# Eight-core layer kernel: the recurrent fronts of the first two tiles run back to back on weights kept in SBUF, with tile two's out-projection placed in the first attention

## The reference, cut to what matters

```python
n  = layernorm(x)
xp = silu(n @ W_in.T)
a  = sigmoid(xp @ W_alpha.T + b_alpha)
b  = sigmoid(xp @ W_beta.T + b_beta)
v  = tanh(xp @ W_v.T + b_v)
h[t] = a[t] * h[t-1] + (b*v)[t]             # a scan over the 4096 tokens
x1 = x + (h * silu(h)) @ W_out.T
n1 = layernorm(x1)
hh = rmsnorm(n1) * gamma1
q  = hh @ Wq + bq ;  k, v = split((hh @ Wdown + bdown) @ Wup + bup)
att = softmax(q_heads @ k_heads.T / 8)      # 16x16, among the heads of one token
u  = n1 + att @ v @ Wo + bo
h2 = rmsnorm(u) * gamma2
g  = softmax(h2 @ Wg + bg)                  # 8 experts, dense
out = x1 + u + sum_e g[e] * (h2 @ We[e])
```

## Time and profile before

| what | value |
|---|---|
| median of 3 runs | 2030.08 us (lowest 2024.43) |
| profiled execution, its own time | 2033.6 us |
| its span, slowest core | 2031.8 us (eight cores: 2020.7 to 2031.8 us) |
| PE busy | 1902.7 us, 94% |
| DVE busy | 1273.2 us, 63% |
| ACT busy | 736.9 us, 36% |
| POOL busy | 219.8 us, 11% |
| HBM read, written | 318.65 MB, 48.23 MB |

### The profile page before, as it was taken

The page is one execution under the profiler, slowest core; times in us unless marked ns, Lnnn a source line. Parts: engine busy times, 40 slices in busy tenths (PEclk is TensorE's granted clock), DMA queues, the critical chain, the costliest instruction groups (busy, mean ns, idle before and its releaser), DMA issues.

```text
span 2031.8 us, 32594 instructions; the slowest of 8 cores (2020.7 to 2031.8 us)
## 1 busy us (share of the span) xinstructions
PE 1902.7 (94%) x11200; PEld 909.7 (45%) x11200; DVE 1273.2 (63%) x2170; ACT 736.9 (36%) x1969; POOL 219.8 (11%) x222
## 2 busy tenths in 40 slices
PE   4666699999999999999999999999999999999899
PEld 2223344445444454455444554444544554444444
DVE  2448546866478646776468665786467764676544
ACT  2226442533434333542325334443335423352200
POOL 4543100120002100020001100021000200011000
PEclk9877799999999999999999999999999999999999
DMA  8999987665533363434543355333543344423344
GB/s 246 301 320 204 152 200 200 163 170 177 192 129 126 124 229 127 161 113 160 203 149 123 120 187 192 108 146 124 208 151 139 125 156 156 145 105 125 125 145 166
DMA packets 49582, 334.89 MB, mean 165 GB/s; under 512 B 6016, under 2 KB 6016, under 8 KB 14592
## 3 DMA queue, kind: packets, MB, share of 16 engines
q1 hardware_dynamic: 42176, 271.45, 38.6%
q0 software_dynamic: 7248, 61.36, 13.4%
HBM read 318.65 MB, written 48.23 MB: 181 GB/s over the span
## 4 chain that ended last, share of the span: by engine, by line
PE 80%; DMA 8%; DVE 7%; issue 3%; ACT 1%; POOL 1%; DVEq 0%; SPq 0%; ACTq 0%; POOLq 0%
PE bank L352 39%; PE bank L407 14%; PE bank L421 6%; PE bank L535 6%; PE bank L392 5%; DVE kt L801 4%; DMA we<-wall 3%; DMA we<-wscr 3%; PE bank L485 2%; DVE R L807 2%; PE bank L520 2%; PE bank L510 1%; PE bank L453 1%; DMA wscr<-wm 1%; PE bank L434 1%
## 5 line engine op out<-in xcount | busy, mean ns | idle before, releaser
L352 PE MATMUL bank<-we,h2T 128*128 128x512 bf16 x4096 | 940.3, 380 | 16.0 <-DMA we<-wscr 7.9
L705 DVE SCALAR_TENSOR_TENSOR xs<-bank,gat,xs 128x512 f32<-128x512 f32 x512 | 384.1, 750 | 411.7 <-PE bank L352 410.3
L352 PEld LDWEIGHTS bank<-we,h2T 128*128 128x128 bf16 x4096 | 385.9, 98 | 441.9 <-issue 29.4
L407 PE MATMUL bank<-F,wm 128*128 128x512 bf16 x1536 | 339.3, 383 | 21.5 <-POOL wm L274 20.6
L287 POOL TENSOR_TENSOR pb<-pb,sml 128x512 bf16<-128x512 bf16 x128 | 133.2, 1040 | 1410.5 <-DVE sml L824 1410.5
L660 ACT ACTIVATE pb<-bank,sml 128x128 bf16<-128x128 f32 x512 | 181.2, 371 | 206.1 <-DVE sml L816 206.1
L407 PEld LDWEIGHTS bank<-F,wm 128*128 128x128 bf16 x1536 | 151.3, 99 | 208.4 <-issue 32.0
L760 DVE SCALAR_TENSOR_TENSOR R<-R 128x512 f32<-128x512 f32 x64 | 47.0, 735 | 123.9 <-ACT R L612 123.9
L421 PE MATMUL bank<-wm,F 128*128 128x512 bf16 x512 | 114.5, 385 | 10.2 <-POOL wm L274 10.2
L453 PE MATMUL bank<-F,wm 128*128 128x512 bf16 x512 | 121.5, 380 | 0.0
L535 PE MATMUL bank<-wm,F 128*128 128x512 bf16 x512 | 113.6, 383 | 0.7 <-DVE F L853 0.7
(11 more groups left out here) (84 smaller groups left out, 1666.0 us busy)
## 6 DMA issues: line engine op xcount, KB each, us to landing
we<-wscr SPq DMA_DIRECT2D x128, 1024.0 KB, 5.2
wm<-wscr SPq DMA_DIRECT2D x98, 1024.0 KB, 5.9
wscr<-wall POOLq DMA_DIRECT2D x16, 1024.0 KB, 15.1
out<-xs SPq DMA_DIRECT2D x32, 512.0 KB, 3.0
wscr<-wm POOLq DMA_DIRECT2D x14, 1024.0 KB, 25.4
xs<-x SPq DMA_DIRECT2D x7, 2048.0 KB, 10.4
xs<-wall POOLq DMA_DIRECT2D x12, 1024.0 KB, 22.9
we<-wall POOLq DMA_DIRECT2D x10, 1024.0 KB, 22.8
```

The source lines that it names most:

```text
L352: mm = pe.matmul(b[:, :], hT[:, kc * 512 + tb * 128:kc * 512 + (tb + 1) * 128], we[ui % NE][:, kc * 512:(kc + 1) * 512], start=(kc == 0), ...
L407: mm = pe.matmul(bk[(mc % 2) * 3 + j][:, :], w[:, (ci % 4) * 1024 + kc * 128:(ci % 4) * 1024 + (kc + 1) * 128], F2[:, kc * 512:(kc + 1) * ...
L705: v.scalar_tensor_tensor(dst, bk[6 + k % 2][:, :], gat[(t - 1) % 2][:, tb * 8 + e:tb * 8 + e + 1], dst, OP.mult, OP.add).then_inc(v_ec, 1)
```

## The change

1. Order. PE, ACT and DVE run t1(0), win(0), abv(0), t1(1), win(1), wout(0), abv(1), wq(0), attention(0), t2(1), wo(0), wdn(1), t3(0), gate(0), and then wq(1), attention(1) and the rest of tile 1 with the experts' units of tile 0 in between. t2(0) and wdn(0) lie inside abv(1). Tiles 2 to 7 keep their order.
2. wout(1), eight groups of eight matmuls, sits in steps j = 0 to 7 of attention(0), with DVE's two instructions of each (`x1ev`) in the same step; the normalization of tile 1 follows in steps 8 to 14.
3. Weights. All 14 units of tiles 0 and 1 are cast once into a buffer of their own (`w0s`: h2T, wm, halves of qt and kt, we[0]) and used for both tiles. Units 0 to 9 are loaded without a wait for PE or for a write-back; units 10 to 13 reuse the buffers of 0 to 3. The write-backs move from POOL to SP and start when unit 9 is cast. Four staging buffers in place of five. x of tile 1 is loaded once unit 0 is cast.
4. `ce(e)` starts after unit 13 and is spread anew, up to `ce(15)` in attention(1).
5. In the fronts of tiles 2 to 7 the 32 transposes on PE and the four copies on DVE are replaced by four DMA transposes on SP's queue, SBUF to SBUF, 128x1024 bf16 each, issued after wo(t-1) and its two weight loads.
6. Three we buffers in place of two (pb and ptv now lie in F2). In wq two units of experts (after mc 2 and 5) in place of one, in wo two in place of three, and in tile 1 sixteen at the end.

The diff, cut to its core:

```diff
-NE = 2
+NE = 3
-A_WIN, A_ABV, A_WOUT, A_T2, A_S0, A_WO, A_T3, A_GATE = 2, 4, 7, 1, 2, 3, 7, 2
+A_WIN, A_ABV, A_WOUT, A_T2, A_S0, A_WO, A_T3, A_GATE = 2, 4, 7, 1, 3, 2, 7, 2
...
+A_END1 = NEC - (A_S0 + A_ATT + A_WO + A_T3 + A_GATE)
...
-    stgh = [xs[2][:, 0:2048], xs[2][:, 2048:4096]] + [t[:, :].bitcast(F32) for t in (h2T[1], we[0], we[1])]
+    stgh = [xs[2][:, 0:2048], xs[2][:, 2048:4096]] + [t[:, :].bitcast(F32) for t in (we[1], we[2])]
+    w0s = [h2T[1], wm[1], wm[2], wm[0], qt[:, 0:4096], qt[:, 4096:8192], kt[:, 0:4096], kt[:, 4096:8192],
+           we[0], h2T[0], h2T[1], wm[1], wm[2], wm[0]]
...
@@ sp_prog
+        def wb(u):
+            sync.wait_ge(c_cm, 2 * u + 2)
+            sync.dma_start(out=wscr[u * 128:(u + 1) * 128, :], in_=w0s[u][:, 0:4096]).then_inc(s_cv[u], 16)
...
+        sync.wait_ge(c_cm, 2)
+        load_x(1)
+        sync.wait_ge(c_cm, 20)
+        for u in range(NMU):
+            wb(u)
...
+        for i in range(NE):
+            load_e(i)
...
             sync.wait_ge(p_wo, t * 8 + 8)
             load_m(m0 + 16)
-            ec(t, A_T3 + A_GATE + A_END)
+            if t + 1 < NT:
+                for b in range(NB):
+                    sync.wait_ge(a_l1a, (t + 1) * 4 + b + 1)
+                    sync.dma_start(out=F1[:, :].rearrange("p (k n) -> p k n", n=TT)[:, :, b * 128:(b + 1) * 128],
+                                   in_=tm1[:, b * D:(b + 1) * D], transpose=True).then_inc(s_t1, 16)
+            ec(t, A_T3 + A_GATE + (A_END1 if t == 1 else A_END))
...
@@ pool_prog
         def cm(u):
-            f = u - NM
-            if f >= 0:
...
-                gp.wait_ge(s_cv[f], 16)
             for hf in range(2):
                 h = 2 * u + hf
-                gp.wait_ge(s_ld[h % 5], 16 * (h // 5 + 1))
-                gp.tensor_copy(wm[u % NM][:, hf * 2048:(hf + 1) * 2048], stgh[h % 5]).then_inc(c_cm, 1)
+                gp.wait_ge(s_ld[h % 4], 16 * (h // 4 + 1))
+                gp.tensor_copy(w0s[u][:, hf * 2048:(hf + 1) * 2048], stgh[h % 4]).then_inc(c_cm, 1)
...
-            gp.dma_start(out=wscr[u * 128:(u + 1) * 128, :], in_=wm[u % NM][:, :]).then_inc(s_cv[u], 16)
...
+        for u in range(10):
+            cm(u)
...
+        gp.wait_ge(p_win, 8 + 4)
+        gp.wait_ge(s_cv[0], 16)
+        cm(10)
...
+        gp.wait_ge(p_abv, 24 + 8)
+        gp.wait_ge(s_cv[3], 16)
+        cm(13)
         ce(0)
+        gp.wait_ge(p_abv, 24 + 16)
         ce(1)
...
@@ pe_prog
+        pe.wait_ge(s_c1, 48)
+        t1(0)
+        win(0)
+        abv(0)
+        t1(1)
+        win(1)
+        for u in range(8):
+            wout(0, u)
+        abv(1)
+        wq(0)
+        att(0)
+        t2(1, range(4))
+        wo(0)
+        wdn(1)
+        t3(0)
+        gate(0)
+        for t in range(1, NT):
+            if t >= 2:
+                win(t)
...
+            wq(t)
+            att(t)
...
+        def att(t):
...
+                if t >= 1:
+                    ec(t, 1)
+                elif j < 8:
+                    wout(1, j)
...
@@ dve_prog
+        def att(t):
...
+                if t == 0 and j < 8:
+                    x1ev(1, j)
+                if j + 1 < 16:
+                    rsum(t, j + 1)
...
+        wo(0)
+        v.drain()
+        xu(0)
+        nb3(0)
+        t3(0)
```

More of the change, by code:

```diff
@@ L689, in act_prog @@
             r.then_inc(a_ge, 1)
+        load_set(SET_LNE)
+        s.wait_ge(v_set, 1)
+        ln1_rstd(0)
+        for b in range(NB):
+            ln1_app(0, b)
+        load_set(SET_SILU)
+        win(0)
+        abv(0)
+        win(1)
+        load_set(SET_LNE)
+        ln2_rstd(0)
+        load_set(SET_SILU)
+        for b in range(NB):
+            ln2_app(0, b)
+        abv(1)
+        load_set(SET_LNE)
+        qv(0)
+        att(0)
+        ln3(0)
+        zev(1)
+        gate(0)
+        for t in range(1, NT):
+            if t >= 2:
+                load_set(SET_SILU)
+                win(t)
+                abv(t)
+                load_set(SET_LNE)
+                ln2_rstd(t)
+                for b in range(NB):
+                    ln2_app(t, b)
+                zev(t)
+            qv(t)
+            att(t)
+            ln3(t)
+            gate(t)
     def dve_prog(v):
@@ new lines, in t3 @@
+        def t3(t):
+            for kc in range(NCH):
+                if kc % 2 == 0:
+                    v.wait_ge(p_t3, t * 4 + kc // 2 + 1)
+                if t < 2 and kc == 0:
+                    v.wait_ge(s_cv[9 + t], 16)
+                bb = bkb[(4, 5, 0, 1)[kc // 2]]
+                v.tensor_scalar_mul(h2T[t % 2][:, kc * 512:(kc + 1) * 512],
+                                    bb[:, (kc % 2) * 512:(kc % 2 + 1) * 512],
+                                    cpf[:, C_G2 + kc:C_G2 + kc + 1]).then_inc(v_t3, 1)
@@ new lines, in dve_prog @@
+        abv(0)
+        t1(1)
+        gmul(0, NCH - 1)
+        for u in range(8):
+            x1ev(0, u)
+        ln2_aggr(0)
+        ln2_nm(0)
+        abv(1)
+        gmul(1, NCH - 1)
+        kv(0)
+        att(0)
+        t2(1, range(NCH))
+        wo(0)
+        v.drain()
+        xu(0)
+        nb3(0)
+        t3(0)
+        gate(0)
+        gates(0)
+        for t in range(1, NT):
+            if t >= 2:
+                ec(t, A_WIN)
+                abv(t)
+                ec(t, 1)
+                gmul(t, NCH - 1)
+                ec(t, A_ABV - 2)
+                for u in range(8):
+                    x1ev(t, u)
+                ln2_aggr(t)
+                ec(t, 2)
+                ln2_nm(t)
+                ec(t, A_WOUT - 2)
+                t2(t, range(NCH))
+                ec(t, A_T2)
+            kv(t)
+            att(t)
+            ec(t, A_WO)
+            wo(t)
+            ec(t, 2)
+            nb3(t)
+            ec(t, A_T3 - 2)
+            t3(t)
+            ec(t, A_GATE)
+            gate(t)
+            ec(t, (A_END1 if t == 1 else A_END) - 1)
+            ec(t, 1)
+            xu(t)
+            gates(t)
```

740 lines of the change are left out of this document (415 added, 325 removed).

## The result

The changed kernel takes 2018.59 us, the median of 11 runs, beside 2030.36 for the kernel before on the same chips; the ratio is 0.9934, 95% interval [0.9908, 0.996]. It is faster, by 12 us or 0.7%, where 52 us were forecast, and inside what counts as no change. The profiled execution spans 2014.3 us, against 2031.8 for the slowest core before.

A forecast was written before the change was run, and what follows sets the result against it. Outside the first tile PE was taken as the bound; there, weight loading, then small matmuls at a low clock. Gains 34.7 + 10.7 + 5.2 + 3 = 53.6 off 2033.6 gave 1980, stated as 1978 us; range 1957 to 2040.

The forecast's parts named there:

- Part 1: Loading and the fronts of tiles 0 and 1: abv(0) ends at 89 us, wout(0) at 123, abv(1) at 168.
- POOL is no bound: Loading in the fronts: POOL's casts, 1.9 us against 3.5 us of transfer a half, do not set the pace.
- Then a tail of 4 us: Between abv(0) and t1(1): ACT's last tanh and two instructions of the next tile's normalization, 4 us.
- abv(1) is 41.6 of matmuls: Second front: abv(1) takes 41.6 us of matmuls plus 4 for t2(0) and wdn(0), ending at 168.
- Part 2: wq(0) and the first attention with the wout filler: attention 73 us, ending at 262; wo(0) done at 282.
- Part 3: From wo(0) to the end of gate(0): wait before t3 grows from 8.7 to 11.7 us; PE through at 299.
- Part 4: Rest of tile 1 after gate(0): 159 us left, tile 2 begins at 458 instead of 492.7, gain 34.7.
- Part 5: Steady tiles: 10.7 us off for t1, 5.2 for kt waits, 3 for expert weights; DMA transposes hidden.
- A: Steady tiles: DMA transposes hold up win(t); gain gone at 6.5 us each, 2100 us at 10 each; chance 0.20.
- B: Loading at the slower rate, 250 GB/s: part of the fronts ends 12 to 14 us later, 1991; with C, 0.24.
- C: First attention's steps 0 to 7 at 1.2 GHz: 56 us instead of 44, total 1991; with B, chance 0.24.

The follow-up runs named there:

- e2: Changed kernel with the weight casts made by the DMA, none on POOL; 2016.87 us, ratio 0.9924 to the kernel before.
- e7: Changed kernel with each POOL cast split into two back-to-back pieces of 128x1024; 2019.92 us, ratio 0.994 to the kernel before.
- e10: Changed kernel with each POOL cast in two pieces, the second waiting for the end of the first; 2013.1 us, ratio 0.987 to the kernel before.
- e1: Changed kernel with tile 0's t2 placed earlier inside abv(1); 2006.34 us, ratio 0.9868 to the kernel before.
- e5: Changed kernel with t2(0) earlier, casts by the DMA and wout(1) before the attention; 1992.42 us, ratio 0.9755 to the kernel before.
- e3: Changed kernel with wout(1) moved out of the first attention to just before it; 2002.85 us, ratio 0.9848 to the kernel before.
- e4: Changed kernel with the input transposes of tiles 2 to 7 back on PE and DVE; 2031.78 us, ratio 0.9999 to the kernel before.
- e9: e5 with gate(2)'s transfer held back until the attention masks have landed; 1996.71 us, ratio 0.9789 to the kernel before.
- e12: e11 with tile 1's first normalization one gate step earlier; 1986.94 us, ratio 0.9778 to the kernel before.
- e11: Changed kernel with t2(0) earlier, wout(1) before the attention and e10's casts; 1988.04 us, ratio 0.9782 to the kernel before.

## Why the prediction was wrong

**Part 1 failed, in three sentences of it.** The stretches behind it were right to within a few us.

*"POOL is no bound: a cast is 1.9 us against 3.5 us of transfer a half."* And after it: *"PE alone would need 27.9 + 14.2 + 41.6 = 84, so the two are nearly in step."* I asked whether POOL keeps up, not what it does to its neighbour, and so the casts' effect on DVE stood in the sum at nothing. In the changed kernel DVE is the engine without slack in most of abv(0), and I did not sum a gate step on it. Shown by e2 (no casts: step 5.2 us, win(1) at 96.3) and, for the kind of contention, by e7 against e10 (same casts, a gap: 9.3 to 7.4). The Trainium skill (SBUF — State Buffer, "Who interferes with whom") says that VectorE and GpSimd share a port pair under an exclusive lock; this trace agrees, and its price here is up to 1.9 us on a scan of 1.28 and on a product of 0.67. (That page of the Trainium skill has the lock held for an instruction; in e7 two instructions without a gap held it like one.) The rate was off as well, on the harmless side: the DMA engines moved 341 GB/s in this stretch, above the 297 that I took and the 334 that I had as its end. The hint was in the trace of before: between 54 and 90 us, with casts further apart, the same scan (there L764) has a mean of 1651 ns:

```profile
L764 DVE TENSOR_TENSOR_SCAN R<-R,hcar 128x512 f32<-128x512 f32 x4 | 6.6, 1651 | 0.3
```

There it showed in no wait of PE: DVE stood idle for 17.5 us of that stretch waiting for ACT, and PE waited for the casts themselves. The change took the idle time away and packed the casts closer: both at once.

*"Then a tail of 4 us".* It was 11.6. In e2 it is 6.25, so 5 of it go with the casts, and 2 were missing in my sum. Together with abv(0)'s 9 us and 1.4 for t1(1) at a slower clock this is the first portion, 18 us on the slowest core; e2 brings 17 of it back there, 10 at the median of the cores.

*"abv(1) is 41.6 of matmuls with t2(0) and wdn(0) inside, 4: 168."* It took 61.8. I counted the matmuls of the moved steps and put the copies between them at nothing, which DVE runs only after gate steps that wait for matmuls behind them in PE's order. The 7.04 and 4.46 us are this ring, some 5 more are matmuls at the lower clock after it. e1 shows it: abv(1) falls by 12 us, the kernel by 12.3. With both causes away (e5) abv(1) took 45.0 us (45.6 summed) and ended at 169.8, so 168 was the right sum for the matmuls alone.

**Part 2 was right in size.** Attention 73.7 for 73, steps 0 to 7 some 47 us for 44. It also said that the filler gains almost nothing, "25 us more for 14 us of matmuls", which by its own numbers is a loss of 11; e3 shows the loss: taking the filler out gave 12.8 us in place and 15.7 in the kernel.

**Part 3 right** (11.7 before t3). **Part 4**: the 159 us behind gate(0) were 161. Its gain of 34.7 did not arrive because the moment it starts from was 36 late. **Part 5 right**: about 233 a tile, the waits for kt and expert weights gone; e4 gives the transposes alone 13 us, for 10.7 summed. That they stayed hidden was in part luck: their landing time of 6.2 us was sized at 3 to 4, and overlap, which I had not counted, made up for it.

**The rivals.** A was the wrong danger, B likewise: loading went faster than forecast. C's lower clock is in the filler (up to 3.4 us for 8 matmuls), but not in all of its steps: 47 us for the eight, between the 44 taken and C's 56. The rival that came true, one engine slowed by another's use of SBUF, was not on the list.

**What stays open.** Why pairs of cores fall to a granted clock of 0.81. In the profiled executions of e2 and e9 it begins near 100 us, where PE becomes dense, and holds to the first attention. No profiled execution of a kernel in which POOL casts shows it in this stretch. But these kernels also start win(1) later (103 us and more, against 96 to 99), and no run separated the two. Nor is it certain that casting DMAs have a part in it: in 15 executions of the kernel before, on three chips, one pair of neighbouring cores had a mean clock of 0.963 to 0.968 (0.971 to 0.977 on the undisturbed others), and most of these pairs ended later than they, by up to 20 us, for instance cores 4 and 5 in the one of 2042.0 us. No trace of these was kept, so whether it is the same level is not known. They raise the median of before in the runs of e9 to e12, and so flatter these ratios. The best kernel by the median is e12, not distinguishable from e11, at 0.978 of before as measured beside it; the two executions of e5 at the full clock were 10 us below, but its executions don't reliably keep it.

## What to carry to other kernels

When a change moves work of one engine closer together, sum the time of the engine next to it as well, with durations from a stretch in which both were busy, and not only whether the moved engine keeps up. For a step moved into another engine's order, follow its hand-overs one by one: which instruction stands ahead of each copy, and does that one wait for something issued behind it? A filler for idle time is worth only its matmuls at the clock of the place where it is put, less what its evictions add to the chain there.

## What the runs showed of the hardware

- A DVE scan of 128x512 float32 takes 1.28 us alone, 3.1 to 3.4 where it meets a cast of 1.90 us on POOL, 2.60 (slowest core of e10) with gaps of 0.1 us inside the casts; the product 0.67, 2.52 to 2.65 and 1.45. Batch statistics (0.68 each) did not change. Halving POOL's instructions without a gap did not shorten DVE's (3.24 and 2.65).
- Two engines that hold each other up can fall into step: in the changed kernel's slowest core a gate step of 8.94 us is three of POOL's rounds of 2.98.
- A third level of the granted clock, 0.81, with 2.27 us for 8 matmuls that take 1.89 at 1.00, on pairs of neighbouring cores. In e9 cores 4 and 5 had it while 6 and 7 of the same die stayed at 1.00. The Trainium skill (TensorE: Matmul & The Clock Gate, "Seeing it yourself") has a clock of 13/16 for peak current, granted by die; 0.81 is that number, but here it took pairs.
- Casting DMAs brought 2 MB of float32 each into SBUF as bf16, one every 6.1 to 6.3 us with three in flight (each landed 16 to 19 us after issue). By an estimate from these numbers that is 330 to 345 GB/s read; the plain loads of the changed kernel came at 1 MB every 2.98 us, 352 GB/s. POOL's part was 0.53 us to issue each.
- DMA transposes of 256 KB landed in 3.1 to 9.4 us and held SP for up to 5.7 us at issue; hidden here, as SP had nothing urgent behind them.
